# Edge aggregation in a graph layer: steps of 256 edges instead of 128, and both message halves in front

## The reference

```python
xn = _layernorm(x)
h_src = (xn @ W_src).reshape(n, 4, 64); h_dst = (xn @ W_dst).reshape(n, 4, 64)
e = a_src[src] + a_dst[dst]; e = where(e > 0, e, 0.2 * e)
p = exp(e - segment_max(e, dst)[dst])
alpha = p / segment_sum(p, dst)[dst]
out = segment_sum(alpha[:, :, None] * h_src[src], dst)      # graph attention
x = x + prelu(layernorm(out + bias)) + mix(xn)              # mix: linear attention over all nodes, then two dense layers
x = x + ffn(layernorm(x))                                   # 8 experts of three dense layers, weighted by a router
```

## Time and profile before

| what | us |
|---|---|
| median of 3 runs (4583.89 to 4587.39) | 4585.84 |
| span of the profiled execution | 5008.5 |
| first stage, up to the first gather | 343.1 |
| first addition to last addition of the middle stage | 448.0 to 3167.1 |
| GpSimd's 1664 gathers, busy | 1775.8 |
| VectorE's 1664 additions, busy | 793.8 |
| TensorE's aggregation products, busy | 1068.5 |

### The profile page before, as it was taken

One profiled execution on the slowest core, in us unless ns is written; L12 is line 12 of the kernel. 1 busy time (PEld: TensorE's weight loads), 2 busy tenths in 40 slices (PEclk: granted clock), 3 DMA queues, 4 the chain that ended last, 5 costly groups with the idle time before them and its releaser, 6 DMA issues. The chain is left out here.

```text
span 5008.5 us, 85791 instructions
## 1 busy us (share of the span) xinstructions
PE 4317.8 (86%) x23103; PEld 3414.7 (68%) x23104; DVE 3827.5 (76%) x9797; ACT 2279.7 (46%) x4346; POOL 1838.8 (37%) x1702
## 2 busy tenths in 40 slices
PE   8973888878888788878877887599999999999999
PEld 7852655555556556555555565388888888888888
DVE  8864777777777777777777787678778877887786
ACT  5531333333333333333333333366666666666666
POOL 2136666666666666666666664000000000000000
PEclk9986899988999898988898898799999999999999
DMA  5544666665666666666665665300000000000000
GB/s 183 172 137 124 176 179 182 193 177 172 179 181 194 179 179 178 175 179 189 179 173 171 178 186 169 110 22 26 26 26 13 26 26 22 17 26 26 19 20 17
DMA packets 440044, 601.74 MB, mean 120 GB/s; under 512 B 41544, under 2 KB 366672, under 8 KB 439888
## 3 DMA queue, kind: packets, MB, share of 16 engines
q1 hardware_dynamic: 360016, 378.46, 23.4%
q0 software_dynamic: 79872, 221.62, 17.5%
HBM read 312.66 MB, written 287.25 MB: 120 GB/s over the span
## 5 line engine op out<-in xcount | busy, mean ns | idle before, releaser
L855 POOL DMA_INDIRECT acc<-h_tab,strips x1664 | 1775.8, 1067 | 1013.5 <-issue 498.6
L989 DVE SCALAR_TENSOR_TENSOR acc<-acc,strips,ps 128x260 f32<-128x260 f32 x1664 | 793.8, 477 | 480.3 <-PE ps L1360 220.8
L1360 PE MATMUL ps<-acc 128*128 128x260 f32 x3328 | 1068.5, 450 | 44.4 <-DVE acc L989 27.3
L1360 PEld LDWEIGHTS ps<-acc 128*128 128x128 f32 x3328 | 647.5, 216 | 157.8 <-DVE acc L989 45.8
L974 DVE TENSOR_TENSOR acc<-acc 128x512 f32<-128x512 f32 x832 | 562.5, 681 | 0.0
L1863 ACT ACTIVATE exp<-ps,bn 128x512 f32<-128x512 f32 (+1 forms) x400 | 310.0, 775 | 492.4 <-PE ps L1930 489.0
L1177 ACT ACTIVATE strips<-ps 128x512 bf16<-128x512 bf16 x416 | 248.0, 596 | 553.9 <-remote 251.5
L1928 PE MATMUL ps<-w_hi,b_hi 128*128 128x256 f32 x1568 | 444.8, 284 | 1.2 <-DVE exp L1767 1.2
L1930 PE MATMUL ps<-w_hi,b_lo 128*128 128x256 f32 x1568 | 443.7, 283 | 0.0
L1929 PE MATMUL ps<-w_lo,b_hi 128*128 128x256 f32 x1568 | 443.6, 283 | 0.0
L1775 DVE TENSOR_TENSOR a_lo<-exp,a_hi 128x512 fp32r<-128x512 f32 (+1 forms) x400 | 261.1, 680 | 169.8 <-ACT a_hi L1865 146.2
(11 more groups left out here) (264 smaller groups left out, 8485.5 us busy)
## 6 DMA issues: line engine op xcount, KB each, us to landing
side_tab<-acc SPq DMA_DIRECT2D x416, 520.0 KB
acc<-h_tab,strips POOLq DMA_INDIRECT x1664
acc<-xnt_tab SPq DMA_DIRECT2D x50, 512.0 KB
h_tab<-proj SPq DMA_DIRECT2D x25, 520.0 KB, 6.6
exp<-side_tab SPq DMA_DIRECT2D x100, 130.0 KB, 2.3
proj<-in_x SPq DMA_DIRECT2D x25, 512.0 KB, 5.3
base_tab<-proj SPq DMA_DIRECT2D x25, 512.0 KB, 3.2
xnt_tab<-proj SPq DMA_DIRECT2D x25, 512.0 KB, 6.0
```

The lines of the kernel that those rows point to most:

```text
L855: pool.indirect_dma_start(G[s][:, b * GU + u], None, h_tab, bass.IndirectOffsetOnAxis(REC[s][:, b * GU + u, 0:1], 0)).then_inc(g_in[s], 16)
L989: nc.vector.scalar_tensor_tensor(A[:, (b % 2) * GU + u], A[:, (k - 1) % (2 * GU) if k else 2 * GU], smt[s][:, k:k + 1], ps[u][:, 0:MW], AL ...
L1360: nc.tensor.matmul(ps[u][:, 0:MW], S32[b % 2][:, u], G[s][:, b * GU + u], start=True, stop=True).then_inc(g_mm.sem, 1)
```

## The change

A step takes 256 edges (`DU` = 2 edge tiles) of one node tile. 782 pairs of tiles and 98 node tiles (`NR`) make 880 steps, 55 groups of `NS` = 16 steps; a batch has `BS` = 2 steps and still 4 gathered tiles. The two products of a step are summed in one PSUM bank, and one addition follows. Banks go round over four steps. The running sums that SyncE writes are two a batch. VectorE's order in a batch becomes: both message halves of batch b + 1, the preparation piece, addition 0, the mixing piece, a one-hot, addition 1. The step tables are half as long; TensorE reads its node tile numbers twice a group instead of four times. The loop ends earlier, so that the last seven groups are written out and groups without a chunk have no mixing piece.

```diff
+DU = 2
+BS = GU // DU
+NS = GS // DU
...
-    TE = -(-E // P)
-    NG = -(-(TE + NT - 1) // GS)
+    TE = -(-E // (DU * P))
+    NR = N // P + 1
+    NG = -(-(TE + NR) // NS)
...
-        A = r3.take(2 * GU + 1, MW)
+        A = r3.take(2 * BS + 1, MW)
...
-                        acc_add.wait(sp, g, GU * (b + 1))
+                        acc_add.wait(sp, g, BS * (b + 1))
...
-                        g_mm.wait(pool, g - 2, GU * (b + 1))
+                        g_mm.wait(pool, g - 2, BS * (b + 1))
...
-                    nc.vector.scalar_tensor_tensor(A[:, (b % 2) * GU + u], A[:, (k - 1) % (2 * GU) if k else 2 * GU],
-                                                   smt[s][:, k:k + 1], ps[u][:, 0:MW], ALU.mult, ALU.add
+                    nc.vector.scalar_tensor_tensor(A[:, k % (2 * BS)], A[:, (k - 1) % (2 * BS) if k else 2 * BS],
+                                                   smt[s][:, k:k + 1], ps[k % 4][:, 0:MW], ALU.mult, ALU.add
                                                    ).then_inc(acc_add.sem, 1)
...
                         if here:
                             if b < GQ - 1:
                                 message(g, s, b + 1, 0)
-                            add(g, s, b, 0)
-                            if b < GQ - 1:
                                 message(g, s, b + 1, 1)
-                            add(g, s, b, 1)
...
                         if here:
+                            add(g, s, b, 0)
                             mix_between(n, s * GQ + b)
-                            add(g, s, b, 2)
...
                         if here:
-                            add(g, s, b, 3)
+                            add(g, s, b, 1)
                             mix_after(n, s * GQ + b)
...
-                    for u in (2 * i, 2 * i + 1):
-                        if b:
-                            acc_add.wait(pe, g, (b - 1) * GU + u + 1)
-                        else:
-                            acc_add.wait(pe, g - 1, (GQ - 1) * GU + u + 1)
-                        nc.tensor.matmul(ps[u][:, 0:MW], S32[b % 2][:, u], G[s][:, b * GU + u], start=True, stop=True
-                                         ).then_inc(g_mm.sem, 1)
+                    if k >= 4:
+                        acc_add.wait(pe, g, k - 3)
+                    else:
+                        acc_add.wait(pe, g - 1, NS + k - 3)
+                    for u in range(DU):
+                        ins = nc.tensor.matmul(ps[k % 4][:, 0:MW], S32[b % 2][:, i * DU + u], G[s][:, b * GU + i * DU + u],
+                                               start=u == 0, stop=u == DU - 1)
+                    ins.then_inc(g_mm.sem, 1)
...
-                            if b in (0, 1, 3, 5):
+                            if b in (0, 3):
                                 fetch(b + 1 if b else 0)
```

More of the change, by code:

```diff
@@ L232, in build @@
         t_at = rt.at
-        t_num = rt.take(STEPS, parts=GS)
+        t_num = rt.take(STEPS * DU, parts=GS)
+        t_parts = t_num.rearrange("p (s u) -> p s u", u=DU)
         j_step = work_t[32:33, t_at:t_at + STEPS].bitcast(i32)
@@ L265, in build @@
         pick = r4.take(GS, parts=GS)
-        smt = [r4.take(GS) for _ in range(2)]
+        smt = [r4.take(NS) for _ in range(2)]
         adb = r4.take(NT * 3 * HEADS // 2, dt=bf16).rearrange("p (j q h) -> p j q h", q=3, h=HEADS)
@@ L324, in build @@
         rs_set, rs_mm, rs_exp, rs_done = stage("rs_set", 5), stage("rs_mm"), stage("rs_exp"), stage("rs_done")
-        msg_set, g_mm, acc_add = stage("msg_set", 2 * GQ), stage("g_mm", GS), stage("acc_add", GS)
+        msg_set, g_mm, acc_add = stage("msg_set", NS), stage("g_mm", NS), stage("acc_add", NS)
         bn_st = stage("bn_st", 2 * (RSQ + 2))
         edge_v = a["edge"].rearrange("t a p -> t (a p)")
-        side_v = side_tab.rearrange("(b u) p c -> b p u c", u=GU)
-        BOUND = "the tables hold edge tiles up to TE and node tiles below NT by their making"
+        side_v = side_tab.rearrange("(b u) p c -> b p u c", u=BS)
+        BOUND = "the tables hold edge tiles up to DU * TE and node tiles below NR by their making"
         LAST_BOUND = "the last step of a node tile lies below STEPS by its making"
         AHEAD = 3
+        REST = NG - 2 * (NCH - 1)
+        assert REST >= AHEAD
+        FETCH = GQ // 2
         def step_values(engine, table, b, most):
-            lo = b * GU
-            sl = table[:, lo:lo + 2 * GU] if isinstance(b, int) else table[:, bass.ds(lo, 2 * GU)]
+            lo = b * BS
+            sl = table[:, lo:lo + FETCH * BS] if isinstance(b, int) else table[:, bass.ds(lo, FETCH * BS)]
             return nc.values_load_multi_w_load_instructions(sl, engines=[engine], min_val=0, max_val=most,
@@ L343, in chunks @@
         def chunks(n):
-            return not (isinstance(n, int) and n >= NCH), not (isinstance(n, int) and n == 0)
+            return not (isinstance(n, int) and n >= NCH), not (isinstance(n, int) and not 0 < n <= NCH)
         def turns(eng, turn, hint):
@@ L353, in body @@
                 turn(g, s, n, q, 1 - s, n + s, None if isinstance(g, int) and g + AHEAD >= NG else g + AHEAD)
-            ring(eng, NG, 2, body, ahead=AHEAD, hint=hint)
+            ring(eng, NG, 2, body, ahead=REST, hint=hint)
         def window(sp, r):
@@ L1059, in mix_between @@
                         statistics(n - 1, 1, 1)
-                    if i == 10:
+                    if (cur or prev) and i == 10:
                         deviations(n)
@@ L1142, in body @@
                          None if isinstance(g, int) and g + AHEAD >= NG else g + AHEAD)
-                ring(dve, NG, 2, body, ahead=AHEAD, hint=True)
+                ring(dve, NG, 2, body, ahead=REST, hint=True)
             @block.scalar
@@ L1533, in fetch @@
                     def fetch(k):
-                        js = step_values(ET.PE, j_step, q * GQ + k, NT - 1)
-                        tiles_of[k], tiles_of[k + 1] = js[0:GU], js[GU:2 * GU]
+                        js = step_values(ET.PE, j_step, q * GQ + k, NR - 1)
+                        for i in range(FETCH):
+                            tiles_of[k + i] = js[i * BS:(i + 1) * BS]
                     def look(k):
@@ L2045 @@
     NP = -(-N // CT) * CT
[L2046 to L2047 removed]
+    TE = -(-E // (DU * P))
+    EP = TE * DU * P
     KC = -(-TE // P)
```

59 lines of the change are left out of this document (31 added, 28 removed).

## The result

The changed kernel takes 4620.9 us (median; 4619.0 to 4623.0) against 4584.9: ratio 1.0079, 95% interval 1.0065 to 1.0093. It is slower, as forecast, but by 36 us and not by 224. Its profiled execution spans 4617.2 us, 4 under the median.

The account below looks back on a forecast made before the run. GpSimd's gathers were taken to set the time of undisturbed runs: fixed parts 2313.5 us plus 1696 gathers at 1.472 us (2496.5) made 4810 us, 4.9% over before. The forecast's own range was 4632 to 4860, the whole range 4560 to 4865.

Parts of the forecast that it names:

- the 96 added ones: GpSimd's gathers in the middle stage: 1760 in place of 1664, priced at 1.409 us each, +135 us.
- The 423 us: Profiled span 5008.5 us over the median 4585.84; taken as the profile's own, late signals in the middle stage.
- the sign that was to show it wrong: GpSimd's gathers: a mean unchanged or lower would mark the forecast wrong; 1110 to 1180 ns was expected.
- messages together: VectorE's paired messages lengthen two-input runs that hold gathers: at most +2.8 us a group, +2.0 taken.
- p = 1.472: Middle stage: forecast time per gather with the change, from 1.409 before; bounds 1.367 and 1.497.
- 18 us²: Sum of squared VectorE run lengths a group before the change; forecast to become 27 to 28, ratio 1.5.
- batch 7: Where two messages already stood together before a 1024-wide operation in every other group; squared sum forecast from 3.7 to 1.6.
- If GpSimd sets the time this is worth nothing: VectorE's additions, 1664 to 880, save it 314 us; claimed worth nothing if GpSimd sets the time.
- Rival A: VectorE and TensorE set the time; VectorE falls 6.4 us a group, about 4490 us; chance 0.21.
- The first gather: Ahead of the gathers: the step table, half as long, was to save about 3 us.
- The tail: From last gather to end of the middle stage, 67.2 us; to shrink by about 15 without mixing work.
- The last stage: TensorE's alone, from 3167 us on; the change does not touch it, kept at 1841.4 us.

Follow-up runs that it names:

- the undisturbed kernel before: The kernel before, no edit, profiled again because its first profile spanned 423 us more than its runs take: 4584.1 us, span 4582.2.
- the run with 28 gathers: The kernel before with 28 instead of 32 gathers a group from the third group on, all other work unchanged: 4571.0 us, ratio 0.9965.
- the hint: The changed kernel with the loop parameter announcing the jump back given to TensorE's last-stage loop: 4600.2 us, ratio 1.0040.
- the kernel before with pairs: The kernel before with both message halves in front of the first addition, steps of 128 edges kept: 4609.0 us, ratio 1.0051.
- the run with each made twice: The changed kernel with every comparison of the step table made twice on VectorE (56 in place of 28): 4620.6 us.

## Why the prediction was off

**Right.** The changed kernel is slower, GpSimd's gathers set its time, and the 96 added ones are its main cost: priced at +135 us, and 134.5 at the pace that the undisturbed kernel before has. The 423 us were the profile's own. The pace for the kernel before, inferred as 1.409 us from a sum over rows of a disturbed trace, was 1.401. Slot waits shrank and ScalarE began to wait for gathers, as foretold. But the time lies under the forecast's own range of 4632 to 4860 us, and the sign that was to show it wrong, a mean of gathers not above 1067 ns, came: 1064.

**The step that failed** is the term "messages together": "a gather that meets operations with two SBUF inputs waits until their unbroken run ends", priced by the sum of squared run lengths. The rule was read from two gathers and made the forecast p = 1.472; measured was 1.369, and 1696 gathers times that difference are 175 us, nearly all of the error. In a group's time (the table's excess divided by 52 and 55 groups), beside the prediction's own price of 5.1 us for 18 us² (2.6 us more a group by the table; it took 2.0):

| | sum of squares | priced, us a group | measured, us a group |
|---|---|---|---|
| batch 7 | 3.7 to 1.6 | -0.6 | 1.78 to 0.22: -1.6 |
| elsewhere | 14.3 to 25.7 | +3.2 | 3.04 to 3.56: +0.5 |

Elsewhere the sign was right and the size six times too large: of the gathers that started 0.15 to 0.5 us after the first of two messages, 107 of 113 were held by that one alone. At batch 7 the saving was nearly three times as large as priced. What the sum left out is that gathers do not come at random: each starts 0.30 us after the last one, and the last one, where it was held, ended 0.82 us after a VectorE operation. So the two engines keep step, and in the kernel before a gather met the longest run at the same place in 24 of 24 cases. Why a gather gets its turn between two messages and not between two others stays open.

On this step the Trainium skill was cited ("SBUF — State Buffer", section "SBUF: two separate sides"), as saying the same. It says that whichever of the two starts first has the port pair for the whole instruction (where VectorE has two SBUF inputs, only against a GpSimd operation that reads SBUF). The traces agree on one side of this: of the 424 gathers over 1.05 us in the kernel before, 420 end 0.79 to 0.85 us after the end of a VectorE operation other than an addition. They differ on the other side. The gather of 2022.91 started first and was held all the same, and of the changed kernel's 880 messages none took more than 0.76 us, however a gather lay beside it. A run of instructions is not in that sentence; the prediction put it there.

**"If GpSimd sets the time this is worth nothing"**, said of the additions, failed as well. Half of them cut short in the kernel before bring 38 us. The gathers' pace fell with them, by 1663 x 0.018 = 29 us, and the rest of the work, within 1% of the gathers, became shorter too (the light group takes 38.6 us in place of 41.0). The prediction's check of its own sum (p = 1.409 from the time of before) could not tell "gathers bind" from "both bind within 1%"; the run with 28 gathers did. Rival A's shorter group came in the light groups only, by 4.2 us in place of 6.4, and the gathers, at 87.6 us a pair of groups, stop it 2 us above the other limit.

**Mis-sized terms.** The first gather: "about -3 us", measured -30. Part is shown: before, GpSimd's 2.4 us operation starts ahead of tile 3's sum on VectorE, and TensorE waits 16.3 us for that sum; changed, the comparison behind it takes the wait and TensorE waits 2.1. Moving the normalization gave 8 of the 30 us at the first gather. By rows and not by a run, the whole wait is 14 us less and the step table's products on TensorE are 8 us less (x65, 15.9 us in all, became x35, 8.0). The other 8 stay open; more comparisons on VectorE don't bring them back. The tail: -15, measured -28. By rows, the last group takes 17.3 us in place of 31.5 from its rescaling to its last addition, which is half of the 28, and no run separates its causes. The last stage: 0, measured +15: where TensorE's last loop lies after the edit, its instructions come late at the jump back in every round, and the hint on that loop takes it away (20 us). That the place is the cause is argued and not shown; two groups more of code in the kernel before did not bring the effect.

The errors sum up: pace after the first 64 gathers -177 (1.368 for 1.472), first gather -27, tail -14, first 64 gathers +8 (87.8 us for 80), last stage +17: -193, from 4810 to the span of 4617.

## What to carry to other kernels

Before an engine is called the bound, take a part of its work away on the chip: here 12% fewer gathers bought 0.3%, since a second limit lay within 1%, and a change that relieves one and loads the other then moves little either way. Before a rule is made from one held gather, count many, and note where in the other engine's order each of them starts: the two engines keep step, so that an average over random arrivals misses both the worst place and the harmless ones. Here the new order saved 95 us at one place and cost 48 at all others. After an edit of one stage, read the others too: here the first stage gave 30 us and the last one, left alone, took 15.

## What the runs showed of the hardware

- A gather that starts 0.15 to 0.5 us after the first of two equal VectorE operations (two SBUF inputs, 0.68 us long, started 0.60 us apart) is mostly held by the first alone: 107 of 113 in the changed kernel, 53 of 67 in the kernel before with pairs. At the pairs of batch 7 this never happened (0 of 18, over three traces). Of gathers that had started from 0.15 us ahead of the first to 0.15 us behind it, in the kernel before with pairs, 27 waited for both, 7 for the first and 7 for neither. What decides was not found.
- Two messages followed by a 1024-wide addition held the gather to the end of all three, and a memset of 0.06 us behind each message changed nothing (longest gather 3.43 us). A gather that starts about 1.0 us after the start of the pair of batch 7 takes 1.11 us where an addition from PSUM follows the pair (changed kernel) and 1.70 where a one-hot does (with the addition back in its old place).
- Gathers did not hold VectorE's messages up (880 of them, none over 0.76 us). GpSimd's operation on 128x1024 elements does hold VectorE, and one tensor input suffices on VectorE's side: a comparison of 128x220 elements beside it took 2.47 us. The Trainium skill, "SBUF — State Buffer", section "SBUF: two separate sides", counts VectorE's operations in a 2-port mode among those that take the pair; the trace agrees, by 2.47 us where 324 ns is the mean of the comparison behind it in the run with each made twice.
- A loop of TensorE with a body of two chunks lost 1.3 to 1.8 us a round at its jump back in one build (140 instruction packets) and nothing in another with the same body (47); the hint removed it (51 packets, 1838.3 in place of 1858.0 us).
